# A layer-norm graph kernel on one core: the diagonal blocks of its projections are cut into 64x64 quarters, and stages of one tile shape are put side by side

## The reference, cut to what matters

```python
def reference(x, adj, bias, W_lang, W_grav, W_V, W_O, gate_logit, log_sigma):  # x: 128 x 64 x 512 f32
    x = layernorm(x + (einsum('bnf,nm->bmf', x, adj * adj) + bias))            # stage "mix"; its result is called h
    z_l, z_g, v = h @ W_lang.T, h @ W_grav.T, h @ W_V.T
    zn  = z_l / norm(z_l)
    A_l = relu(zn @ zn.T) * not_eye                        # per batch, 64 x 64
    A_g = exp(-dist2(z_g) / (2 sigma^2)) * not_eye         # needs z_g @ z_g.T
    K   = w * rowstochastic(A_l * adj) + (1 - w) * rowstochastic(A_g * adj)
    return layernorm(h + (K @ v) @ W_O.T)
```

## Time and profile before

| | us |
|---|---|
| median of 3 runs | 585.32 |
| lowest and highest | 584.85, 588.26 |
| profiled execution, its own time | 587.0 |
| span of the profiled execution | 585.2 |
| PE busy in the span | 567.0 (97%) |
| DVE busy | 479.2 (82%) |
| ACT busy | 355.6 (61%) |
| POOL busy | 212.8 (36%) |

### The profile page before, as it was taken

The page is one execution under the profiler, slowest core; times in us unless marked ns, Lnnn a source line. Parts: engine busy times, 40 slices in busy tenths (PEclk is TensorE's granted clock), DMA queues, the critical chain, the costliest instruction groups (busy, mean ns, idle before and its releaser), DMA issues.

```text
span 585.2 us, 14906 instructions
## 1 busy us (share of the span) xinstructions
PE 567.0 (97%) x5753; PEld 286.7 (49%) x5753; DVE 479.2 (82%) x1027; ACT 355.6 (61%) x670; POOL 212.8 (36%) x230
## 2 busy tenths in 40 slices
PE   9899799999999999999999999999999999999993
PEld 6544545445454545445454545445454545445451
DVE  1667769797998889797988889797988889797765
ACT  2477655666767575666767575666767574634432
POOL 0142432626243342626242442626252433504021
PEclk9999899999999999999999999999999999999998
DMA  8863240354535244253535233253535231314103
GB/s 219 246 131 73 46 100 13 63 145 73 143 63 139 49 106 90 55 143 72 143 65 142 52 103 86 55 142 72 143 70 142 48 99 19 73 55 75 72 2 143
DMA packets 89658, 55.19 MB, mean 94 GB/s; under 512 B 71072, under 2 KB 71072, under 8 KB 89632
## 3 DMA queue, kind: packets, MB, share of 16 engines
q1 hardware_dynamic: 89632, 54.84, 38.9%
HBM read 21.27 MB, written 16.78 MB: 65 GB/s over the span
## 4 chain that ended last, share of the span: by engine, by line
PE 90%; DVE 4%; DMA 2%; ACT 1%; SPq 1%; issue 0%; POOL 0%; POOLq 0%; ACTq 0%
PE proj L449 35%; PE proj L467 28%; PE ps_t L481 8%; PE front L420 4%; PE ps_v L496 3%; PE ps_t L505 3%; PE ps_k L546 2%; PE front L546 2%; PE proj L670 2%; DMA o<-in_L_gnn_W_O 2%; PE ps_v L526 1%; DVE stats L919 1%; DVE p_lo L951 1%; PE ps_t L670 1%; DMA ht_lo<-h_lo 1%; SPq L345 1%
## 5 line engine op out<-in xcount | busy, mean ns | idle before, releaser
L1334 POOL TENSOR_TENSOR x_lo<-x_in,x_hi 128x512 f16<-128x512 f32 x60 | 75.2, 1265 | 121.3 <-ACT x_hi L699 121.3
L709 ACT ACTIVATE p_hi<-proj 128x512 f16<-128x512 f32 x128 | 76.0, 594 | 62.3 <-PE proj L449 62.0
L467 PE MATMUL proj<-m_hi,ht_hi 128*64 128x512 f16 x512 | 98.9, 383 | 0.0
L467 PE MATMUL proj<-m_lo,ht_hi 128*64 128x512 f16 x512 | 97.9, 379 | 0.0
L467 PE MATMUL proj<-m_hi,ht_lo 128*64 128x512 f16 x512 | 97.9, 379 | 0.0
L951 DVE TENSOR_TENSOR p_lo<-proj,p_hi 128x512 f16<-128x512 f32 x128 | 87.4, 683 | 6.8 <-ACT p_hi L709 5.1
L714 ACT ACTIVATE uv<-proj 128x512 f16<-128x512 f32 x64 | 38.1, 596 | 53.4 <-PE proj L467 53.4
L449 PE MATMUL proj<-ht_hi,l_grav_hi 128*128 128x512 f16 x160 | 61.1, 382 | 0.5 <-DVE p_lo L951 0.5
L449 PE MATMUL proj<-ht_hi,l_lang_hi 128*128 128x512 f16 x160 | 61.0, 381 | 0.6 <-DMA ht_lo<-h_lo 0.6
L449 PE MATMUL proj<-ht_hi,l_grav_lo 128*128 128x512 f16 x160 | 60.6, 379 | 0.0
L449 PE MATMUL proj<-ht_lo,l_lang_hi 128*128 128x512 f16 x160 | 60.6, 379 | 0.0
(11 more groups left out here) (213 smaller groups left out, 1251.4 us busy)
## 6 DMA issues: line engine op xcount, KB each, us to landing
x_in<-in_x SPq DMA_DIRECT2D x32, 512.0 KB, 7.1
out<-o SPq DMA_DIRECT2D x15, 1024.0 KB, 5.2
w_raw_lang<-in_L_gnn_W_lang SPq DMA_DIRECT2D x4, 256.0 KB, 3.4
o<-in_L_gnn_W_O SPq DMA_DIRECT2D x1, 1024.0 KB, 10.4
w_raw_grav<-in_L_gnn_W_grav SPq DMA_DIRECT2D x4, 256.0 KB, 10.2
uv<-in_L_gnn_W_V SPq DMA_DIRECT2D x1, 1024.0 KB, 13.7
ht_hi<-h_hi SPq DMA_TRANSPOSE x64, 2.5
ht_lo<-h_lo SPq DMA_TRANSPOSE x64, 2.5
```

Of the source, the lines that this page charges most:

```text
L467: mm = pe.matmul(proj[j % 3][q * N:(q + 1) * N, :], a[g.parity][:, k, rows:rows + N], b[:, k, :], start=(n == 0), stop=(n == len(passes) - 1))
L709: act.activation(p_hi[:, j % 4, :, j // 4, :], by_batch(proj[j % 3]), ACT.Copy).then_inc(phi_ready, 1)
L1334: pool.tensor_tensor(x_lo[:, p, :], x_in[g.parity][:, p, :], x_hi[:, p, :], ALU.subtract).then_inc(xlo_ready, 1)
```

## The change

1. The diagonal block of each unit keeps its hi*lo pass as a full 128x128 matmul. Its hi*hi and lo*hi passes are cut into 64x64 quarters. T is symmetrised later anyway, so of the two off-diagonal quarters one is left out and the other is taken whole: the factors on the four quarters (`half_of`) are 0.5, 0.5, 1 and 0. Three quarters for each of 4 blocks and 2 passes are 24 quarters for a side, in `diagonal_blocks(g, side)`. Some quarters must run on the other half of the rows than that in which their data lie, so SP's queue makes copies with the halves swapped: `ht_turn` by two DMAs for each group (`turn`), `l_turn` once by 20 DMAs (`turn_weights`).
2. The units of one side now end together, so a side needs four banks at a time: `unit_bank = [proj0, proj1, proj2, ps_t, ps_k, proj0, proj1, proj2]`. `kernel_t` and the banks of `attend` and `values` move accordingly; `attend` is preceded by one matmul of one column (`attend_gate`).
3. The order on PE becomes: mix 0, units 0 to 3, diagonal blocks of lang, mix 1, units 4 to 7, `kernel_t`, diagonal blocks of grav, `attend_gate`, attend 0 and 1, values 0, gram, `third_norm` (the old `x_norm(third)`), values 1, 2, 3, spread, symmetrise.
4. The orders on DVE, ACT and POOL are written anew. On DVE `x_sum(third)` stands behind `diagonals(g)`, `out_stats(before, 1)`, `squared_norms(g)` and `out_stats(before, 2)` and `(before, 3)`; on ACT `x_squares(third, 3)` stands behind `t_copy(g)` and `h_high(nxt, 2)`.

```diff
+        ht_turn = sb("ht_turn", [P, DC - 1, ROWS], F16)
+        l_turn = sb("l_turn", [P, 2, 2, DC - 1, P], F16)
-        ku_bank = [ps_k, *front, ps_t]
-        last_ku_bank = [ps_k, *front, proj[0]]
+        ku_bank = [ps_t, *front, ps_v]
+        last_ku_bank = [*front, ps_k, proj[0]]
+        unit_bank = [*proj, ps_t, ps_k, *proj]
+        value_bank = [ps_k, *proj]
+        x_norm_start, x_norm_bank = ps_v[:, XN:XN + 1], front[0][:, 0:1]
...
+            def turn(g):
+
+                sp.wait_ge(ht_hi_loaded[g.parity], g.half * 64 + 64)
+                if g is not groups[0]:
+                    sp.wait_ge(proj_done, g.prev().count(12, 8))
+                sp.dma_start(ht_turn[L, 0:2, :], ht_hi[g.parity][GR, 0:3:2, :]).then_inc(ht_turned, 16)
+                sp.dma_start(ht_turn[GR, :, :], ht_hi[g.parity][L, 1:4, :]).then_inc(ht_turned, 16)
...
+            def project(g, j, first, mixed=None):
...
+                elif j < 3:
+                    pe.wait_ge(ulo_ready, g.prev().count(4, j + 2))
+                if j > 4:
+                    pe.wait_ge(plo_ready, g.count(8, j - 4))
+                passes = [(c, l_hi, ht_lo)] + [(k, a, b) for k in range(c + 1, DC)
+                                               for a, b in ((l_hi, ht_hi), (l_hi, ht_lo), (l_lo, ht_hi))]
+                if j == 3:
+                    pe.wait_ge(ht_turned, g.count(32, 32))
...
+                    if mixed:
+                        mix_waits(mixed, 1)
...
+            def diagonal_blocks(g, side):
+
+                s = ("lang", "grav")[side]
+
+                def quarter(c, rows, cols, part, turned=None):
+                    w, x = (l_hi, l_lo)[part][s][rows, blk(c, c), cols], ht_hi[g.parity][rows, c, :]
+                    if turned is not None:
+                        w, x = l_turn[rows, side, part, turned, cols], ht_turn[rows, turned, :]
+                    return pe.matmul(unit_bank[4 * side + c][cols, :], w, x, start=False, stop=True, skip_group_check=True)
+
+                for part in range(2):
+                    quarter(0, L, L, part)
+                    quarter(1, GR, GR, part)
+                    quarter(1, GR, L, part, turned=0)
+                    quarter(0, L, GR, part, turned=0)
+                for part in range(2):
+                    quarter(0, L, L, part, turned=0)
+                    quarter(3, GR, GR, part)
+                    quarter(1, GR, L, part)
+                    mm = quarter(2, L, GR, part, turned=1)
+                mm.then_inc(proj_done, 2)
+                for part in range(2):
+                    quarter(3, L, L, part)
+                    quarter(3, GR, GR, part, turned=2)
+                    quarter(2, GR, L, part, turned=1)
+                    mm = quarter(2, L, GR, part)
+                mm.then_inc(proj_done, 2)
...
+            def attend_gate(g, before, nxt):
+
+                pe.wait_ge(ktlo_ready, before.count(1, 1))
+                pe.wait_ge(ulo_ready, before.count(4, 4))
+                pe.wait_ge(plo_ready, g.count(8, 4))
                 if nxt:
-                    pe.wait_ge(y_ready, nxt.count(4, 3 + a))
+                    pe.wait_ge(y_ready, nxt.count(4, 4))
+                pe.matmul(ps_v[:, 0:1], ones16[:, :], ones16[:, 0:1], start=True, stop=True, skip_group_check=True)
+
+            def third_norm(g, third, first):
+
+                pe.wait_ge(xsum_ready, third.prev().count(1, 1))
+                if first:
+                    pe.wait_ge(xbase_ready, 2)
+                    pe.wait_ge(y_ready, g.next().count(4, 3))
+                else:
+                    pe.wait_ge(sum_ready, g.prev().count(4, 2))
+                x_norm(third, x_norm_bank)
...
+                project(g, 3, first, mixed=nxt)
+                diagonal_blocks(g, 0)
+                if has_next:
+                    mix(nxt, 1)
+                project(g, 4, first)
+                project(g, 5, first)
+                project(g, 6, first)
+                project(g, 7, first)
+                if has_prev:
                     kernel_t(before)
-                project(g, 5, first, (before, 0, nxt) if has_prev else None)
+                diagonal_blocks(g, 1)
                 if has_prev:
+                    attend_gate(g, before, nxt)
                     attend(before, 0, ku_bank)
-                project(g, 6, first, (before, 1, nxt) if has_prev else None)
-                if has_prev:
                     attend(before, 1, ku_bank)
-                project(g, 7, first)
-                if first:
+                if has_next:
+                    if not first:
+                        values(g, 0)
                     gram(g, first)
-                    values(g, 0, first)
+                    if first:
+                        values(g, 0, first)
+                    if has_square:
+                        third_norm(g, third, first)
                     values(g, 1)
-                elif has_next:
-                    values(g, 0)
-                    gram(g, first)
-                    values(g, 1)
-                if has_next:
                     values(g, 2)
-                    if has_square:
-                        pe.wait_ge(xsum_ready, third.prev().count(1, 1))
-                        if first:
-                            pe.wait_ge(xbase_ready, 2)
-                        x_norm(third)
                     values(g, 3)
-                    spread(g, first, third)
-                    symmetrise(g, split)
+                    spread(g, first)
+                    symmetrise(g, split, third)
```

The new order on ACT, second half of an iteration:

```diff
                 p_high(g, 6, first)
                 if has_square:
                     x_squares(third, 0)
+                    x_squares(third, 1)
                 p_high(g, 7, first)
...
                 if has_next:
                     h_high(nxt, 0)
+                    if has_split and not first:
+                        x_scaled(split, 2)
+                    if has_prev:
+                        u_high(g, 0)
+                    if has_split and not first:
+                        x_scaled(split, 3)
+                    if has_square:
+                        x_squares(third, 2)
                     h_high(nxt, 1)
+                    t_copy(g, first)
...
                     h_high(nxt, 2)
+                    if has_square:
+                        x_squares(third, 3)
+                    h_high(nxt, 3)
```

The new order on DVE, from the last unit of a group on:

```diff
                 p_low(g, 7)
+                if has_next:
+                    if has_prev:
+                        residual(before, 1, False)
+                    h_low(nxt, 0)
+                    norm_rows(nxt, 1, before)
...
+                    if has_prev:
+                        residual(before, 2, False)
+                        residual(before, 3, False)
+                    norm_rows(nxt, 2, before)
+                    h_low(nxt, 1)
+                    norm_rows(nxt, 3, before)
+                    if has_prev:
+                        out_stats(before, 0)
+                        u_low(g, 0)
+                    diagonals(g)
+                    if has_prev:
+                        out_stats(before, 1)
+                    squared_norms(g)
+                    if has_prev:
+                        out_stats(before, 2)
+                        out_stats(before, 3)
+                    if has_square:
+                        x_sum(third)
+                    shifted(g)
```

More of the change, by code:

```diff
@@ L409, in mix_waits @@
                     pe.wait_ge(h_ready, g.prev().count(4, 4))
+                    if third:
+                        pe.wait_ge(xbase_ready, third.prev().count(1, 1))
                 else:
@@ L1183, in iteration @@
+                    u_low(g, 1)
+                    u_low(g, 2)
+                    if has_prev:
+                        out_shift(before)
+                    similarities(g)
+                    if has_square:
+                        x_inverse(third)
+                else:
+                    residual(before, 1, False)
+                    residual(before, 2, False)
+                    residual(before, 3, False)
                     out_stats(before, 0)
-                if has_next:
-                    h_low(nxt, 0)
-                    norm_rows(nxt, 3, before)
@@ L1376, in iteration @@
                 split = g.next().next() if has_split else None
-                third = split.next() if has_square else None
                 if first:
@@ L1380, in iteration @@
                     x_back(split)
-                    ln1(nxt)
+                third = split.next() if has_square else None
+                if has_split and not first:
                     x_low(split, 0)
                     x_low(split, 1)
-                else:
-                    if has_split:
-                        x_low(split, 0)
-                    if has_next:
-                        ln1(nxt, split)
+                if has_next:
+                    ln1(nxt)
+                if first:
+                    x_low(split, 0)
+                    x_low(split, 1)
```

(8 more changed lines are left out.)

317 lines of the change are left out of this document (145 added, 172 removed).

## The result

The changed kernel takes 677.95 us in the median of 6 runs (676.08 to 680.49), against 587.21 for 6 runs of the kernel before beside it (584.85 to 588.26): a ratio of 1.155, 95% interval 1.152 to 1.159.

The account below looks back on a forecast made before the run. PE bounds the kernel, busy 567.0 of 585.2 us. Adding 12 x (-1.3 + 5.2 + 1.7) = 67.2, -2.6 for iterations 13 and 14, -1 for the end, +5 for iteration 0 and 0.2 for the start gave 654 us, range 630 to 678.

Parts of the forecast that it names:

- the wait on x_sum: PE at third_norm behind gram, iterations 1 to 12: a wait of 5.2 us each, ends 5.0 and 5.9.
- the half clock: Behind each such wait PE runs 3.4 us at 1.2 GHz, losing 1.7 us; ends 0.5 and 3.4.
- the tail: End of the program: iteration 14 put at 1.3 us less, iteration 15 and what follows at 1 less.
- PE alone: A steady iteration without waits: 31.5 us on PE instead of 32.82.
- What the quarters save: Quarters and new order on PE: 0.86 us from passes, 0.46 from shape changes, 0.02 back for the gate, 1.3 less.
- its 13: Changes of tile shape per steady iteration in the new order, 17 before; four fewer at 0.115 us save 0.46.
- The page's rule: Different row tiles cannot access one PSUM bank simultaneously; the last 8 quarters of a side do so.
- the rival built on it: Quarters don't run by four, by shared bank or order: 0.86 us an iteration, 14 in all, 668 us; chance 0.13.
- The covered waits: Swapped copies, attend_gate and gram's last p_low: taken as 0 us; gate and gram priced from 0 to 0.5 an iteration.
- The wait that is not covered: Chain from gram through t_copy, t_diagonal, diagonals and DVE's queue to x_sum: 5.0 us, plus 0.2 for DVE late.
- the two-stretch rival: Two slow clock stretches behind each wait: 12 x 1.7 us more, 674 us; chance 0.08.
- Iteration 0 and the ends: Iteration 0 waits at third_norm, unit 3 and gram: +5 us, ends 0 and +9; iterations 13 and 14 gain 1.3 each.

Follow-up runs that it names:

- norm_late: The changed kernel with only third_norm moved back behind values 2: 585.07 us, ratio 0.997.
- before_norm_early: The kernel before with only x_norm moved right behind gram, in all iterations but the first: 656.90 us, ratio 1.121.
- factors_early: The changed kernel with third_norm directly ahead of spread, x_base behind u_low 2, and squared_norms, inverse_norm and diagonal_matrices moved ahead: 574.95 us, ratio 0.980.
- wait_filled: The changed kernel with 26 full passes that nobody reads ahead of third_norm, in iterations 1 to 12: 651.95 us, ratio 1.112.
- sum_early: The changed kernel with x_squares 3 moved ahead of t_copy on ACT and x_sum ahead of h_low 1 on DVE: 581.23 us, ratio 0.992.

## Why the prediction was right in its mechanism and short in its size

The forecast was 654, the result 678; the profiled span, to which the sum was made, 676.3. In the loop two steps failed, both in the size of a term: the wait on x_sum was put at 5.2 us and is 6.0, and the half clock at 1.7 us and is 2.2. Outside of it the tail, put at 2.3 us less, is 2.2 us more. The sign and the cause are shown: the wait of third_norm for x_sum is on the trace as written down, norm_late takes the whole loss away, and before_norm_early makes it without the rest of the change. The steps, as the prediction put them, for each of iterations 1 to 12:

| term | forecast | measured | from |
|---|---|---|---|
| PE alone | 31.5 | 31.6 | factors_early 31.61 |
| wait on x_sum | 5.2 | 6.0 | 225.98 to 232.03, 6.02 to 6.06 in all twelve |
| half clock | 1.7 | 2.2 | wait_filled against the mean of after |
| iteration | 38.4 | 39.8 | |

- **What the quarters save.** The term -1.3 measured -1.2, where no wait stands in the way: 0.66 for the quarters and 0.55 for the order. Its parts were divided otherwise than forecast: 0.86 for the quarters is nearly right for the passes alone (0.41 a side), but on the side of grav they bring a change of shape of their own, a dearer one than the others (0.17). The prediction had that change in its 13, so the sum came out within 0.1.
- **The page's rule, and the rival built on it.** The last eight quarters of a side run four at a time, in steps of 0.21 to 0.22 us, though both row halves write one bank. The rival's 0.86 us are nowhere. The Trainium skill (TensorEngine Tiling (Array Packing), Gotcha 1: PSUM Pressure) excludes simultaneous access of different row tiles to one bank; here, on different partitions of it, the measurement decides against that.
- **The covered waits** held in the loop: the turned copies, the gate, and gram.
- **The wait that is not covered: the first failed step.** The links were right, their sum was 0.9 us too short: +0.3 for t_diagonal, which took 1.28 in the earlier trace rows and 1.59 here, and +0.6 for squared_norms, put at 0.31 and taking 0.93 (229.71 to 230.64). Both durations were read beside other work of POOL and DVE than stands there in the new order: squared_norms begins at 229.71, while POOL's second h_low is under way, and ends as that ends. Another 0.06 lie between x_sum's end and the matmul, and the 0.2 us by which DVE was to be late were nil: diagonals (228.51) began as t_diag ended (228.48). So 5.0 became 6.0, just beyond the end of 5.9.
- **What the idle time does to the clock: the second.** One slow stretch of 3.4 us behind a wait of 3.0 was the only row, and a wait of 3.8 in before_norm_early mostly buys the same. A wait of 5.9 buys 6.8 us, behind 11 of the 12 (behind the other one, and behind the 2.5 of iteration 0, it is 3.4); part of it is spent within the wait, 0.9 to 3.9 us where it is that long, and 2.2 us are lost in the mean, not the 3.4 of the two-stretch rival. So that rival had the stretch right and its price wrong; its 674 was near the time for a partly wrong reason, with the longer wait making up the difference.
- **Iteration 0 and the ends.** +6.4 for +5 in iteration 0: third_norm waits 2.5 us, not half as long as in the loop, and gram waits 4.5 us for 3.0; slow stretches of 6.8 and 3.4 us go with the two, where before had one of 3.4. Iteration 13 gained 0.6 and not 1.3, and the tail lost 2.2 where 2.3 were to be gained. In the last iteration PE asks 2.7 us too early for the bank that DVE's residual 1 reads, and 3.4 us at half clock follow. In the kernel before, all four residuals stand ahead of the last p_low on DVE (the fourth starts at 555.21, p_low at 555.87); in the new order attend stands behind all the units, and residuals 1 to 3 behind the last p_low. This can be read from the order of the change; the prediction gave the part one sentence.

The differences add up: 16.3 for the 12 iterations (83.5 - 67.2), 1.4 for iteration 0, 0.7 for iteration 13, 4.5 for the tail, -0.7 for the start, 22.2 of the 22.3 us between 654.0 and 676.3.

## What to carry to other kernels

Before a matmul is moved forward to save a change of shape (0.10 us), ask what its operand waits for on the other engines: here the operand stood behind work that could only begin when the instruction just ahead was over, and two changes of shape saved cost 8.2 us. On an engine that is never idle otherwise, a wait can cost more than its length: here the clock fell to half behind each wait of 3.8 or 5.9 us, which cost another 2.2 us an iteration in the changed kernel. While such a wait of PE can't be avoided, independent passes belong into it. And when a wait is removed, look where the next operand stands before the gain is booked: the one for x_sum hid one ahead of spread, and in the last iteration the one for a residual hid another. The same chain, from gram over ACT, POOL and DVE, is behind both x_sum and spread.

## What the runs showed of the hardware that was not expected

**A short DVE instruction can last as long as POOL's.** squared_norms works on 64x8 numbers. In sum_early, where POOL is idle beside it, it takes 0.20 us (median 0.21 of 16); in the changed kernel 1.01 (median of 16), ending at 230.72, when POOL's h_low ends (230.70); in the kernel before 0.39, again with its end 0.02 us behind that of POOL's h_low. The timeline of DVE in sum_early:

```profile
300.65 0.20 DVE L1039 TENSOR_SCALAR nsq<-diag,eps_nsq 64x8 f32<-64x8 f32 x1
```

r_sb, on the chain to spread, behaves likewise: 0.70 us in the kernel before, 1.53 in the later ones, and it ends 0.54 to 0.55 us behind POOL's instruction beside it in both (272.26 and 272.81 before; 300.04 and 300.58 in factors_early). Not all of DVE's work is held up: in the changed kernel diagonals and out_stats keep their 0.69 and 0.68 us beside the same h_low of POOL (228.51 and 229.11). That squared_norms and r_sb wait for POOL is argued from these ends, no experiment removed POOL's instruction alone. The Trainium skill (SBUF — State Buffer, SBUF: two separate sides) says that DVE and GpSimd share a pair of ports as an exclusive lock, held for a whole instruction, and that DVE takes part in it in a 2-port mode or with two inputs in SBUF. These rows agree with that: squared_norms can be of the first kind (which mode it runs in isn't shown), r_sb is of the second.

**The fall of the clock comes late and lasts beyond its cause.** In the iteration shown PE idled for 5.1 us at the full 2.4 GHz, and of the 6.8 us at 1.2 GHz 5.9 lay over the work that followed; in before_norm_early, whose waits are shorter, the fall came only when PE was at work again in 5 of the 12 iterations. With 26 useless passes in the wait the granted clock stayed at 1.00.

**Row halves that write one PSUM bank at different partitions** start side by side, in steps of 0.21 to 0.22 us, like quarters with a bank for each half.
